# Two attention layers' openings and last slots rearranged: key rows, key tiles, mask branch, score banks, copies

## The chip, the cores and the metric

One core of one Trainium2 chip runs the kernel in one launch. The metric is the device time of an execution in microseconds; lower is better. Within an execution the hardware profiler's trace gives every instruction's start and length.

## The reference

Four residual steps over x of 8 batches x 256 tokens x 128 features, in float32:

```
x = x + attention_0(layernorm(x), ctx, ctx)       # 16 heads of 8 features, with biases, softmax
x = x + experts(layernorm(x))                     # top-1 of 8 experts, 128 -> 512 -> 128, silu, times the gate
x = x + attention_1(layernorm(x), ctx, ctx)       # no biases; scores get -slope[h] * (pos_q - pos_k), and
                                                  # -inf where mask == 0; e = exp(s - max s); e / (1 + sum e)
x = x + spikes(layernorm(x))                      # relu(x Wfc)^2 Wproj, 5 steps of a threshold, counted / 5
```

The mask of the inputs is all ones; the kernel tests it when it runs and has code for both cases.

## The kernel before

Every engine has one instruction stream, written out by hand, and semaphores order them. An attention layer is a loop of slots s = -3 .. 8 (`slots_loop`, L299), one batch of 256 tokens entering per slot and each batch spread over several slots: in slot s batch s+3 is normalized, batch s+2 gets its queries (and, in layer 0, keys), batch s+1 gets the first score pass, batch s the second score pass and its value products, and batch s-1 its division, output product and addition to X. `new`, `nxt`, `cur`, `old` in the code are these. A slot has eight pairs of heads (`pair(i)`, L428).

The first score pass (`p1`, L347) has query rows on partitions; VectorE takes each row's maximum from PSUM (`reduce`, L805, L809, 16 a batch). The negated maxima are split into parts, turned by TensorE (`m_turn`, L408), copied (`m_copy`, L667, to `mT`) and put by a DMA of SP into rows 3, 7, .. of the query tile (`rows_of_maximum`, L1047), so that the second pass (`p2`, L355), with key rows on partitions, yields scores less the maximum. ScalarE takes the exponential from PSUM (L664, 16 a batch), and TensorE multiplies by the values (`pv`, L396, 4 groups of 16 products). Then `o_copy` (L646), transposes to token rows (L454), the division on VectorE (`o_norm`, L822), the transpose of the result (L487), its copy `aT` (L714), the output product (L503) and the addition to X (L913).

Queries and keys are float16 high and low parts: ScalarE writes the full product and the high part, GpSimd or VectorE the low part, and SP's DMAs copy them to rows of `Qt` and `Kt` (three tiles each, `NBUF`). Row block 3 of `Kt` is a constant (clear, then add of a column of `rows`), row block 3 of `Qt` partly too (`q_const`). In layer 0 all this is done in the slots; at the opening the first keys' high part is issued by ScalarE (L643), and `Kt[1]` and `Kt[2]` are cleared and filled by VectorE (L799, L802). SP waits for `inited` (L1057) in slot -1 before it loads the next part of the context and touches those tiles.

PSUM has eight banks: `R` with six, three for the first pass (`row_bank`) and three for the second (`key_bank`), and `M[0]`, `M[1]` for everything else. In the last slot of a layer (s = 7) there is no first pass.

Layer 1's keys and values are computed ahead: for batches 0 to 2 before the experts, for 3 to 6 after them (`ahead_on_tensor`, L556), for 7 in slot -2. The parts go to HBM by SP (L593, L598) and come back as whole key tiles. After the experts TensorE reads a flag that says whether any mask value is zero, and takes one of two branches, each with the whole attention of layer 1 (L1748 to L1754).

`keep_running` (L333) issues 128x512 products that nobody reads; `FILLS` and several places give their number. After attention 1 the last step runs as `ffn` slots s = -3 .. 7: h of batch s+2, transposes of batch s+3, y of batch s+1, spikes of batch s. Slots -3 and -2 stand inside the attention's last slots (`ffn_start`), the rest behind it (`ffn_loop`). Its normalization's statistics come in parts (`FFN_PARTS`).

## Time and profile before

| | |
|---|---|
| three runs, us | 370.54 (median), 370.26, 373.01 |
| the profiled execution's own time, us | 372.42 |
| its span in the trace, us | 370.5 |
| granted TensorE clock, mean over the span | 0.934 |
| busy: TensorE, VectorE, ScalarE, GpSimd | 86%, 75%, 63%, 40% |
| chain that ended last: TensorE, VectorE, issue, ScalarE, DMA | 44%, 22%, 11%, 11%, 8% |
| VectorE's reductions L809 | 256 x 684 ns = 161.7 us of the engine, 16% of the chain |

Shares of busy time are means over stages. By the trace attention 0 lies from 0 to about 131 us, gate and routing to 148, the experts to 202, attention 1 to 337, and the last step's slots from 331 to 370. TensorE's granted clock is 1.00 (2.4 GHz) or 0.50 (1.2 GHz); a mean between them says for what part of a stretch each held. ACTq, SPq and PEq are the engines' queues, in which DMA issues and register loads stand.

### The profile page before, as it was taken

Reading aid. Unit: us, or ns where it says so; the run is one execution under the profiler, and the core shown is the slowest. Engines: PE = TensorE matmul, PEld = TensorE weight load, DVE = VectorE, ACT = ScalarE, POOL = GpSimd, SP = SyncE. Lnnn points to the kernel's source line nnn. Section 1 sums busy time; section 2 is a strip of 40 time slices with the busy share of each in tenths; the row PEclk is TensorE's granted clock in tenths of the full one; section 3 lists DMA queues with packets and bytes.
Section 4 is the critical chain, followed back from the end, with each engine's and each line's share of the span. In section 5 each row is a group of like instructions: output and inputs, shape, how many; then the busy total and the mean of one; then the engine's idle time right before and its main releaser. Section 6 shows DMA issues by size and latency. Waiting matters only on the chain.

```text
span 370.5 us, 9195 instructions
## 1 busy us (share of the span) xinstructions
PE 318.3 (86%) x3235; PEld 188.7 (51%) x3235; DVE 278.8 (75%) x693; ACT 233.3 (63%) x524; POOL 146.4 (40%) x227
## 2 busy tenths in 40 slices
PE   5798889889988866899998597899988998898993
PEld 2333444444443465599898342344444443347993
DVE  5699999999993648455672339999999998604676
ACT  2138988998888424345555211698898986845652
POOL 3244635366300312875420578355434310354500
PEclk9899999999998876899999788999999996879999
DMA  4224343452422053255551332121221120000111
GB/s 170 71 75 115 105 109 104 112 144 54 152 65 60 3 140 97 50 140 152 134 132 39 96 95 63 51 54 31 66 66 54 25 54 7 6 2 1 36 37 42
DMA packets 33118, 27.89 MB, mean 75 GB/s; under 512 B 4544, under 2 KB 27968, under 8 KB 33072
## 3 DMA queue, kind: packets, MB, share of 16 engines
q1 hardware_dynamic: 30960, 24.07, 22.9%
q0 software_dynamic: 1248, 2.56, 3.2%
q10 hardware_dynamic: 864, 0.66, 0.6%
q8 instruction: 28, 0.46, 0.5%
q14 instruction: 18, 0.15, 0.1%
HBM read 14.75 MB, written 5.70 MB: 55 GB/s over the span
## 4 chain that ended last, share of the span: by engine, by line
PE 44%; DVE 22%; issue 11%; ACT 11%; DMA 8%; POOL 2%; ACTq 0%; SPq 0%; DVEq 0%; POOLq 0%
DVE nm L809 16%; PE M L403 13%; ACT Pt L664 7%; PE R L349 6%; PE R L1613 4%; DMA Pt<-in_mask 3%; PE M L1631 3%; PE R L1445 3%; PE R L358 3%; PE R L1428 2%; PE M L336 2%; DMA sorted_y<-ysb 2%; PE M L503 1%; ACT Osb L648 1%; PE R L336 1%
## 5 line engine op out<-in xcount | busy, mean ns | idle before, releaser
L809 DVE TENSOR_REDUCE nm<-R 128x2 f32<-128x512 f32 x256 | 161.7, 684 | 8.6 <-PE R L349 7.3
L664 ACT ACTIVATE Pt<-R 128x512 f32<-128x512 f32 x256 | 140.2, 596 | 32.9 <-PE R L358 31.6
L403 PE MATMUL M<-Pt,Vt 128*32 128x256 f32 x1024 | 73.2, 407 | 0.3 <-ACT Pt L664 0.3
L349 PE MATMUL R<-Kt,Qt 32*128 32x256 f16 x512 | 50.9, 277 | 13.2 <-DVE nm L809 11.7
L358 PE MATMUL R<-Qt,Kt 32*128 32x256 f16 x512 | 52.1, 281 | 2.6 <-ACT Pt L664 2.3
L1473 ACT ACTIVATE hf<-R,small_in 128x128 f32<-128x128 f32 x92 | 26.3, 367 | 27.9 <-PE R L1428 27.8
L349 PEld LDWEIGHTS R<-Kt,Qt 32*128 32x128 f16 x512 | 14.6, 93 | 54.8 <-DVE nm L809 44.0
L403 PEld LDWEIGHTS M<-Pt,Vt 128*32 128x32 f32 x1024 | 27.8, 114 | 26.6 <-ACT Pt L664 9.1
L1333 POOL DMA_INDIRECT xt<-normed_x,source x23 | 22.8, 992 | 17.2 <-PE M L1436 11.5
L1428 PE MATMUL R<-x_t,w_t 128*128 128x128 f32 x184 | 25.6, 282 | 0.6 <-DVE x_t L1496 0.5
L336 PE MATMUL M<-ones 128*128 128x512 f16 x65 | 22.3, 458 | 3.9 <-issue 3.9
L1445 PE MATMUL R<-w_ff,hf 128*128 x184 | 24.4, 277 | 0.9 <-DVE ysb L1502 0.9
L1340 POOL DMA_INDIRECT w_ff<-sorted_y,slot x16 | 15.4, 966 | 21.0 <-DMA sorted_y<-ysb 16.7
L1445 PEld LDWEIGHTS R<-w_ff,hf 128*128 128x128 f32 x184 | 22.4, 192 | 1.3 <-issue 1.2
L1428 PEld LDWEIGHTS R<-x_t,w_t 128*128 128x128 f32 x184 | 22.3, 192 | 1.3 <-issue 1.0
L685 ACT ACTIVATE xnT<-M 128x256 f32<-128x256 f32 x16 | 6.2, 387 | 22.0 <-PE M L467 18.9
L358 PEld LDWEIGHTS R<-Qt,Kt 32*128 32x128 f16 x512 | 15.3, 93 | 8.6 <-ACT Pt L664 5.6
L1502 DVE COPY ysb<-R 128x128 f32<-128x128 f32 x23 | 6.7, 290 | 17.1 <-PE R L1446 11.9
L771 POOL TENSOR_SCALAR xn<-X,mv,rstd 128x128 f32<-128x128 f32 x24 | 19.0, 797 | 1.3
L987 POOL CAST q_hi<-qf 128x256 f16<-128x256 f32 x12 | 4.8, 398 | 36.8 <-ACT qf L699 21.0
L336 PE MATMUL R<-ones 128*128 128x512 f16 x46 | 16.9, 505 | 2.3 <-DVE ones L1720 1.2
L778 POOL TENSOR_SCALAR ve<-mv 128x2 f32<-128x2 f32 x16 | 3.8, 235 | 35.0 <-DVE mv L755 35.0
(191 smaller groups left out, 526.3 us busy)
## 6 DMA issues: line engine op xcount, KB each, us to landing
w_ff<-in_w SPq DMA_DIRECT2D x8, 512.0 KB, 4.0
Pt<-in_mask SPq DMA_DIRECT2D x8, 256.0 KB
Kt<-k_rows SPq DMA_DIRECT2D x8, 256.0 KB, 2.8
Qt<-q_hi SPq DMA_DIRECT2D x30, 64.0 KB, 1.9
k_rows<-Pt SPq DMA_DIRECT2D x24, 64.0 KB
sorted_y<-ysb SPq DMA_DIRECT2D x23, 64.0 KB
Qt<-q_const SPq DMA_DIRECT2D x16, 64.0 KB, 3.5
Qt<-q_lo SPq DMA_DIRECT2D x16, 64.0 KB, 1.9
```

Source lines behind the costliest of these rows:

```text
L336: pe.matmul(bank, ones16[:, :], ones16[:, :].unsqueeze(1).to_broadcast([P, 4, P]), start=True, stop=True)
L349: mm = pe.matmul(row_bank(b, h)[:, q, :], Qt[b % NBUF][rows_of(h), h // HG, q * P:(q + 1) * P], Kt[b % NBUF][rows_of(h), h // HG, :], star ...
L358: mm = pe.matmul(key_bank(b, 2 * pair + hh)[:, k, :], Kt[b % NBUF][rows_of(h), h // HG, k * P:(k + 1) * P], Qt[b % NBUF][rows_of(h), h // ...
L403: mm = pe.matmul(o_bank(b)[KB * i:KB * i + KB, tile * S:(tile + 1) * S], Vflat[par][:, at:at + KB], Pt[g][:, i, k * S:(k + 1) * S], start= ...
L664: act.activation(Pt[i // 2][:, 2 * j + hh, :], key_bank(b, 2 * i + hh).rearrange("p k n -> p (k n)"), ACT.Exp, scale=1.0 / SC).then_inc(ly ...
L771: i = pool.tensor_scalar(xn[par][:, q, :], X[:, b * QT + q, :], mv[:, q, 0:1], rstd[:, q:q + 1], ALU.subtract, ALU.mult)
L809: v.tensor_reduce(nm[par][:, h // 8, :, h % HG, h // HG % 2], row_bank(b, h), AX.X, ALU.max, negate=True)\
L1333: pool.indirect_dma_start(xt[j % XT_BUFS][:, :], None, xn_dram, bass.IndirectOffsetOnAxis(ap=source[:, j:j + 1].bitcast(U32), axis=0)) \
L1340: pool.indirect_dma_start(yg[:, i, :], None, ys_dram, bass.IndirectOffsetOnAxis(ap=slot[:, i:i + 1].bitcast(U32), axis=0)) \
L1428: mm = pe.matmul(S2[j % H_BUFS // 2][:, j % 2, c // 2, (c % 2) * P:(c % 2 + 1) * P], w1_t[j % X_BUFS][:, c, :], x_t[j % X_BUFS][:, :], sta ...
L1445: pe.matmul(o, hf[j % HF_BUFS][:, c * P:(c + 1) * P], second_weights(e, c), start=(c == 0), stop=False)
L1473: i = act.activation(hf[j % HF_BUFS][:, c * P:(c + 1) * P], S2[j % H_BUFS // 2][:, j % 2, c // 2, (c % 2) * P:(c % 2 + 1) * P], ACT.Silu, ...
```

## The change

SP issues all of layer 0's first key rows, after the first key tile is made, and ScalarE issues the first constant query rows instead; the additions that make `q_const` and `vb` change places. GpSimd clears and fills `Kt[1]` and `Kt[2]`, and SP waits for that in slot -1. VectorE computes the first low query part before it normalizes batch 1. Fewer fillers run in slot -2 of both layers. In slot 7 the second pass uses five banks, and pairs 6 and 7 stand before value groups 0 and 1; `o_copy`, the second `m_copy` and the `aT` copy of that slot (in layer 1 those of slot 8 too) are done by VectorE. Layer 1's ahead products of batches 3 to 6 stand inside the branches; SP issues the first constant query rows before the stores of batches 3 and 4, and the stores of 5 and 6 behind the first queries. The bias addition of slots 0 and later stands before the normalization on GpSimd. The last step's statistics come in parts of 2, 4, 1 and 1 batches instead of 6, 1 and 1, and its slot -1 moves into attention slot 8.

```diff
@@ L215
-INIT_KEYS, INIT_TILES, INIT_SECOND, N_INIT = 11, 14, 18, 20
+INIT_KEYS, INIT_KT, INIT_Q, INIT_TILES = 11, 12, 13, 14
@@ L325
+LAST_RING = (4, 5, 3, 1, 2)
-    return R[:, RING + (H * b + n) % RING, :, :]
+    return R[:, LAST_RING[n % len(LAST_RING)] if b == B - 1 else RING + (H * b + n) % RING, :, :]
+def on_vector(ly, b):
+    return b == B - 2 or b == B - 1 and ly["position"]
@@ L388
-            if b > 0 or i >= 1:
+            if b == B - 1:
+                pe.wait_ge(ly["exp_done"], H * b + (2 * i - 3 if i >= 2 else i - 1))
+                if i == 1:
+                    pe.wait_ge(ly["max_done"], H * B)
+            elif b > 0 or i >= 1:
@@ L426
+            pe.wait_ge(inited, INIT_TILES)
@@ L456
+        if ffn and s == B:
+            ffn_start(ffn, -1)
-            keep_running(pe, M[1][:, :], 16)
+            keep_running(pe, M[1][:, :], 10)
@@ L482
-            keep_running(pe, spare, 12)
+            keep_running(pe, spare, 8)
@@ L535
+            if s == B - 1:
+                pair(6)
-        pair(6)
+        if s != B - 1:
+            pair(6)
+        else:
+            pair(7)
-        if ffn and s == B - 1:
+        if s != B - 1:
+            pair(7)
+        elif ffn:
-        pair(7)
@@ L639
-    if b == -2:
-        act.wait_ge(ly["k_hi"], 1)
-        act.wait_ge(inited, INIT_TILES)
-        for block in (0, 2):
-            act.dma_start(Kt[0][block:P:4, :, :], k_hi[:, :]).then_inc(ly["k_rep"], 16)
@@ L674
-        if old:
+        if old and not on_vector(ly, b - 1):
-        if cur:
+            ffn_start(ffn, -1)
+        if cur and s != B - 1:
@@ L686
+        if s == -2 and ly["bias"]:
+            act.wait_ge(inited, INIT_Q)
+            act.dma_start(Qt[0][3:P:4, :, :], q_const[:, :, :]).then_inc(ly["q_tile"], 16)
@@ L710
-        if old:
+        if old and not on_vector(ly, b - 1):
@@ L734
+        exp(7)
-        exp(7)
@@ L791
+    v.tensor_scalar(q_const[:, :, :], q_const[:, :, :], rows[0:KB, 1:2], None, ALU.add).then_inc(inited, 1)
-    v.tensor_scalar(q_const[:, :, :], q_const[:, :, :], rows[0:KB, 1:2], None, ALU.add).then_inc(inited, 1)
-    for i in range(1, NBUF):
-        v.memset(Kt[i][:, :, :], 0.0).then_inc(inited, 1)
-    v.wait_ge(inited, INIT_SECOND)
-    for i in range(1, NBUF):
-        v.tensor_scalar(Kt[i][:, :, :], Kt[i][:, :, :], rows[:, 0:1], None, ALU.add).then_inc(inited, 1)
@@ L834
+    def o_copy(b, par):
+        v.wait_ge(ly["pv_done"], NG * (b + 1))
+        if b >= 2:
+            v.wait_ge(ly["ot_done"], b - 1)
+        v.tensor_scalar(Osb[par][:, :, :].rearrange("p t n -> p (t n)"), o_bank(b)[:, :],
+                        rows[:, 2:3] if ly["position"] else 0.0, None, ALU.add).then_inc(ly["o_copied"], 1)
+    def last_m_copy():
+        v.wait_ge(ly["mT_done"], 2 * B)
+        v.wait_ge(ly["m_rows"], 16 * (2 * B - 2))
+        v.tensor_copy(mT[1][:, :], M16[0][0:2 * KB, 0:S]).then_inc(ly["mT_copied"], 1)
+    def a_copy(b):
+        v.wait_ge(ly["aT_done"], b + 1)
+        v.wait_ge(ly["op_done"], b)
+        v.tensor_copy(aT[:, :], M[1][:, 0:S]).then_inc(ly["aT_copied"], 1)
@@ L852
+        if old and on_vector(ly, b - 1):
+            o_copy(b - 1, 1 - par)
+        if s == B - 1:
+            last_m_copy()
@@ L865
+            if s == -2 and ly["bias"]:
+                v.wait_ge(ly["q_hi"], 1)
+                v.wait_ge(ly["q_copied"], 1)
+                v.tensor_tensor(q_lo[par][:, :], qf[:, :], q_hi[par][:, :], ALU.subtract).then_inc(ly["q_lo"], 1)
@@ L875
-            if s == -2:
+            if s == -2 and ly["position"]:
-                if ly["bias"]:
-                    v.wait_ge(ly["q_copied"], 1)
-                    v.tensor_tensor(q_lo[par][:, :], qf[:, :], q_hi[par][:, :], ALU.subtract).then_inc(ly["q_lo"], 1)
-                else:
-                    v.scalar_tensor_tensor(q_lo[par][:, :], M[0][:, 0:S], QK / float(np.sqrt(DH)), q_hi[par][:, :],
-                                           ALU.mult, ALU.subtract).then_inc(ly["q_lo"], 1)
-                if ly["position"]:
-                    ahead_on_vector(v, KV_LAST, B)
+                v.scalar_tensor_tensor(q_lo[par][:, :], M[0][:, 0:S], QK / float(np.sqrt(DH)), q_hi[par][:, :],
+                                       ALU.mult, ALU.subtract).then_inc(ly["q_lo"], 1)
+                ahead_on_vector(v, KV_LAST, B)
@@ L901
+        if old and on_vector(ly, b - 1):
+            a_copy(b - 1)
+        if ffn and s == B - 1:
+            ffn_stats(v, 1)
@@ L918
-            ffn_stats(v, s - B + 2)
+            ffn_stats(v, s - B + 3)
@@ L935
+def clear_keys(pool):
+    for i in range(1, NBUF):
+        pool.memset(Kt[i][:, :, :], 0.0).then_inc(cleared, 1)
+    pool.wait_ge(loaded, 16 * N_LOADS)
+    pool.wait_ge(cleared, 4 + NBUF - 1)
+    for i in range(1, NBUF):
+        pool.tensor_scalar(Kt[i][:, :, :], Kt[i][:, :, :], rows[:, 0:1], 0.0, ALU.add, ALU.add).then_inc(cleared, 1)
@@ L978
+                clear_keys(pool)
@@ L996
+        if s >= 0 and nxt and ly["bias"]:
+            pool.wait_ge(ly["ob_made"], 1)
+            pool.tensor_tensor(X[:, (b + 1) * QT:(b + 2) * QT, :], X[:, (b + 1) * QT:(b + 2) * QT, :],
+                               ob[:, :].unsqueeze(1).to_broadcast([P, QT, D]), ALU.add).then_inc(ly["x_biased"], 1)
-        if nxt and ly["bias"]:
+        if s < 0 and nxt and ly["bias"]:
@@ L1040
-        if b > -2:
-            sp.dma_start(tile[block:P:4, :, :], k_hi[:, :]).then_inc(ly["k_rep"], 16)
+        sp.dma_start(tile[block:P:4, :, :], k_hi[:, :]).then_inc(ly["k_rep"], 16)
@@ L1057
-            sp.wait_ge(inited, N_INIT)
+            sp.wait_ge(cleared, 4 + 2 * (NBUF - 1))
@@ L1073
-            sp.dma_start(tile[3:P:4, :, :], q_const[:, :, :]).then_inc(ly["q_tile"], 16)
+            if s != -2:
+                sp.dma_start(tile[3:P:4, :, :], q_const[:, :, :]).then_inc(ly["q_tile"], 16)
@@ L1085
+            if s == -2 and ly["position"]:
+                for j in range(KV_EARLY + 2, KV_LAST):
+                    ahead_high_on_sync(sp, j)
+                    ahead_low_on_sync(sp, j)
@@ L1399
-    for j in range(KV_EARLY, KV_LAST):
+    sp.dma_start(Qt[0][3:P:4, :, :], q_const[:, :, :]).then_inc(ly[1]["q_tile"], 16)
+    for j in range(KV_EARLY, KV_EARLY + 2):
@@ L1538
-FFN_PARTS = (0, B - 2, B - 1, B)
+FFN_PARTS = (0, 2, B - 2, B - 1, B)
-    for s in range(-1, B):
+    for s in range(B):
@@ L1594
-        if b in (1, 4):
-            ffn_root(pool, 1 if b == 1 else 2)
+        if b in (2, 3, 5):
+            ffn_root(pool, (2, 3, 5).index(b) + 1)
-        pool.wait_ge(ff["rstd"], 2 if b < FFN_PARTS[1] else 2 * b - 2 * FFN_PARTS[1] + 4)
+        pool.wait_ge(ff["rstd"], 2 * sum(b >= start for start in FFN_PARTS[1:]) + 2)
@@ L1626
+                pe.wait_ge(ly[1]["o_copied"], B)
+            if s == 0:
@@ L1674
-    sp.wait_ge(inited, INIT_TILES)
+    sp.wait_ge(inited, INIT_KT)
@@ L1747
-    ahead_on_tensor(pe, KV_EARLY, KV_LAST)
+        ahead_on_tensor(pe, KV_EARLY, KV_LAST)
+        ahead_on_tensor(pe, KV_EARLY, KV_LAST)
```

## Rows read from the trace of the kernel before

**Rows 1.** Windows, a middle slot: us; busy PE, PEld, DVE, ACT, POOL; clock; DMA.

```profile
51.00:63.00 12.00, 10.88 (x152) 5.29 (x144) 11.76 (x25) 10.83 (x24) 4.87 (x9) 1.00 0.42 124
```

**Rows 2.** Timeline of layer 0's opening: start us, us, engine, line, what, count.

```profile
6.71 0.44 PE L467 MATMUL M<-first_in,xn 128*128 128x128 f32 x2 [0.66 <-DVE xn L761]
...
8.14 1.51 ACTq L643 DMA_DIRECT2D Kt<-k_hi  x2
...
9.70 0.38 ACT L685 ACTIVATE xnT<-M 128x256 f32<-128x256 f32 x1 [3.05 <-issue]
...
10.91 0.18 POOL L934 MEMSET Vt<- 128x32 f32 x1
...
14.53 0.34 SPq L1029 DMA_DIRECT2D ctxT<-in_ctxT  x1
...
15.69 1.29 DVE L809 TENSOR_REDUCE nm<-R 128x2 f32<-128x512 f32 x2 [1.18 <-PE R L349]
...
20.55 0.70 PE L492 MATMUL M<-ctxT,first_in 128*128 128x256 f32 x2 [0.16 <-ACT qf L699]
```

**Rows 3.** DMA issues from 14.5 to 15.5 us, with size and us to landing.

```profile
ctxT<-in_ctxT SPq DMA_DIRECT2D x1, 128.0 KB, 2.4
```

**Rows 4.** Groups of GpSimd by form: count, busy us, mean ns, idle time before.

```profile
L771 POOL TENSOR_SCALAR xn<-X,mv,rstd 128x128 f32<-128x128 f32 x24 | 19.0, 797 | 1.3
...
L1266 POOL MEMSET b2rows<- 128x1024 f16 x1 | 1.0, 951 | 0.0
...
L1281 POOL TENSOR_SCALAR pos_r<-pos_f,small_in 128x256 f32<-128x256 f32 x1 | 0.5, 476 | 0.1
...
L1267 POOL TENSOR_SCALAR brest<-small_in 128x8 f32<-128x8 f32 x1 | 0.2, 202 | 0.1
```

**Rows 5.** Windows in layer 0's last slot, columns as in rows 1.

```profile
112.00:116.00 4.00, 3.00 (x36) 1.33 (x28) 0.78 (x2) 3.94 (x9) 0.00 (x0) 1.00 0.18 24
...
120.00:122.00 2.00, 2.00 (x24) 0.54 (x17) 1.97 (x13) 0.62 (x2) 0.00 (x0) 0.50 0.03 8
```

**Rows 6.** Timeline of layer 0's last two slots.

```profile
110.30 1.07 PE L403 MATMUL M<-Pt,Vt 128*32 128x256 f32 x16
...
118.52 0.42 DVE L913 TENSOR_TENSOR X<-M,X 128x256 f32<-128x256 f32 x1 [3.47 <-PE M L503]
...
118.95 1.94 PE L403 MATMUL M<-Pt,Vt 128*32 128x256 f32 x16
...
123.33 2.62 POOL L1140 TENSOR_TENSOR rstd_all<-ve_all,mhalf 128x14 f32<-128x14 f32 x1
```

**Rows 7.** Instructions on tile mask_any: TensorE's register load, ns and start.

```profile
L1749 PEldq TENSOR_LOAD <-mask_any x1: 413/413/413, 204.8 to 204.8; - x1
```

**Rows 8.** Chain of waits from 195 us on: start us, us, what.

```profile
205.99 3.95 issue
```

**Rows 9.** Timeline of layer 1's opening.

```profile
202.41 0.16 DVE L1321 TENSOR_SCALAR mask_any<-R 128x1 int32<-128x1 f32 x1 [0.47 <-PE R L1326]
...
209.73 0.62 DVE L1515 SCALAR_TENSOR_TENSOR X<-w_ff,gate,X 128x128 f32<-128x128 f32 x2 [4.35 <-DMA w_ff<-sorted_y,slot]
...
216.33 0.38 PE L467 MATMUL M<-first_in,xn 128*128 128x128 f32 x2
...
229.52 0.71 POOL L991 TENSOR_TENSOR q_lo<-qf,q_hi 128x256 f16<-128x256 f32 x1
...
231.38 0.56 SPq L1052 DMA_DIRECT2D Qt<-mT  x1
...
233.64 0.39 PE L349 MATMUL R<-Kt,Qt 32*128 32x256 f16 x4
```

**Rows 10.** Windows in layer 1's last slot, columns as in rows 1.

```profile
320.00:322.00 2.00, 0.85 (x9) 0.35 (x8) 1.06 (x8) 1.94 (x5) 1.44 (x2) 0.93 0.07 16
...
328.00:330.00 2.00, 2.00 (x29) 0.73 (x22) 0.00 (x0) 0.92 (x4) 0.84 (x2) 0.86 0.00 0
```

**Rows 11.** Timeline of the last step's first products.

```profile
331.56 2.00 PE L1613 MATMUL R<-gT,spiking_in 128*128 128x256 f32 x8
```

## The prediction

> **What bounds the kernel now.** I read the page's slices first, then the windows by stage, then the timeline and the chain of waits around the four places that the change touches. In a middle slot of either attention layer VectorE bounds the work: it is busy 11.76 of 12 us, with the clock at full [rows 1]. Nothing of the change shortens its 16 reductions, so the middle stays as it is. What is left are the two openings and the two last slots, which stand in series with the middle; a microsecond there is a microsecond of the total.
>
> Layer 0's opening: ScalarE issues the two high-key transfers at 8.14, and its copy of the transposed tokens, ready since 7.15, starts only at 9.70; VectorE's first reduction starts at 15.69, just behind twelve fillers on TensorE [rows 2]. The last slots: TensorE is busy 3.00 of 4 us from 112 to 116, with the clock at full, and from 120 to 122 it has half [rows 5]; in layer 1 it has half from 321.72 (0.93 on average over two us, of which 0.85 busy) to 328.56 (0.86 over two us) [rows 10]. Sixteen value products take 1.94 us then, against 1.07 [rows 6]. Layer 1's opening: TensorE's branch, 3.95 us without work after 205.99, then sixteen fillers up to the transposes at 216.33 [rows 8, 9].
>
> **The change part by part.**
>
> *Layer 0's opening.* Without the two issues in its queue ScalarE copies at about 7.2 instead of 9.70, issues one constant transfer behind it (0.7 us, beside TensorE's product), and all that follows is 2.5 us earlier. The low query part now stands ahead of the normalization on VectorE; the order costs nothing, since the root that it waits for comes no sooner. SP takes over two issues and drops one; it starts when the key tile is ready, one microsecond earlier, and is done before the query's high part is. With the query there 2.5 us sooner and four fillers fewer, which ended last, the reductions start at 12.3: 3.4 us earlier. Now the other side. Two clears and two additions for key tiles 1 and 2 go to GpSimd, behind its values clear (ends at 11.09), and SP waits for all of them before the second context part, which it issues at 14.53 before the change [rows 2]. A clear of this size is 0.95 us. The addition has no row. Nearest is one with the same operands (one scalar from a tile, one constant) over 256 columns, 476 ns, against 202 ns for 8: 1.1 ns a column, so 1.33 us for 1024 columns. Far bounds: 0.95 us, as the clear; and 5.3 us, at the rate of the normalization, 797 ns for 128 columns with two scalars from tiles [rows 4]. I take 1.33: GpSimd ends at 11.1 + 1.9 + 2.7 + 0.2 for gaps = 15.9. SP issues the context then, and it lands 2.4 us later [rows 3], at 18.3. The key product, at 20.55 before and else at 17.1, waits for it, and the rest of the slot behind it [rows 2]. Gain 20.55 - 18.3 = **2.2 us**. At 0.95 us it is 3.0; at 5.3 us the context lands at 26.3 and the slot loses 5.7. Also queued behind the clears is GpSimd's root for batch 2, which follows them at once and stands in no later chain than the key product.
>
> A rule speaks against this part. The Trainium skill, GPSIMD Engine Reference, section "Performance versus the Vector engine", has 512 elements in 769 ns for a tight loop and keeps elementwise work on VectorE; an estimate by it, 1.54 us an addition, makes this gain 1.8 us instead of 2.2. No row here has this operation at this size.
>
> *The bias add* moves ahead of the root on GpSimd, in time in which it waits for VectorE's moments: nothing. Without that cover it would cost its own 0.7 us a slot, but on GpSimd, which is no bound there: it is busy 4.87 of 12 us [rows 1].
>
> *Layer 0's last slot.* Five score banks instead of three let TensorE run two pairs ahead; three copies leave ScalarE, whose 16 exponentials (9 us) remain. VectorE has no reductions there. Its 128x512 copy has no row; two reductions over the same input take 1.29 us [rows 2], twice the 128x256 addition 0.84 [rows 6]: 0.7, against ScalarE's 0.60, so the rows of the maxima leave 0.25 us later. The order is then: transposes at 113.6, normalization at 114.4, attention transposes at 115.25, copy by 116.2, output product (0.7 us at full clock) by 117.3, addition to X at 117.4 instead of 118.52 [rows 6]. TensorE would end its last value products some 3 us sooner with the clock at full. But behind that stand VectorE's statistics (unchanged) and GpSimd's root, 2.62 us from 123.33 [rows 6], which hold the gate's normalizations and so the last batch. They gain 118.52 - 117.4. I take **1.2 us**; 0 if the clock falls again.
>
> *Layer 1's opening.* The flag is known at 202.57; its load into TensorE's queue stands at 204.8 now, while products run, and ends 4.7 us before the first filler at 209.94 [rows 7 to 9]. The change puts four batches of key products behind the branch. The load then ends at 203.0 and the products start at 203.0 + 4.7 = 207.7, not 202.4. The clock was at half when work came back from the last gap (sixteen fillers took from 209.94 to the transposes at 216.33), so I price them at 1.8 times, as the value products show [rows 6]: four batches took 3.6 us up to 205.99, so two take 3.3 and are done near 211.1 (209.5 at full clock) instead of 204.2. VectorE's low parts of these two stand ahead of its add for batch 0, which goes from 209.73 to 212.5 [rows 9]. Ten fillers instead of sixteen hide what the batches lose: the transposes come near 216, no loss. But GpSimd's root, twelve gathers and its low query part for batch 1 follow that add in order: 229.52 becomes 232.4 [rows 9]. The low part then lands at 235 and the rows of the maxima, issued at 231.38 before, at 236.1, while slot 0's first products stand at 233.64 [rows 9]. Half a microsecond of slack goes first, and VectorE had two reductions left to do; the loss is **1.8 us**. Bounds: none if the key products run at full clock and the code is there sooner (a gain of 0.6 through the transposes), 3 us if all of it stays at half. SP's constant transfer comes earlier; six store issues of 0.6 us move behind the query's low part, where SP waits for the next high part anyway.
>
> *Layer 1's last slot and the tail.* The same five banks and copies. VectorE normalizes statistics of 4 tiles first instead of 12, so they no longer hold its o-normalization. With the clock at full the 6.84 us at half [rows 10] hold 3.8 us of work: 3.0 less, and 0.4 of lulls. Last value products end near 328.2; the first FFN product was at 331.56 [rows 11]. One further FFN slot moves ahead of the attention's last transposes. It fills lulls around these transposes and makes new ones behind ScalarE's relu and VectorE's copy; an estimate is 0.3 us for it, 0 and 1 being its bounds. The tail behind is unchanged. **3.7 us**; 0.4 if the clock falls again.
>
> Sum: -2.2 - 1.2 + 1.8 - 3.7 = -5.3. The profiled execution took 372.42 us around a span of 370.5; it would take 367.1. That is 1.88 above the median of the three runs, 370.54. Against the median: **365.2 us**.
>
> **The rivals.**
>
> *The clock falls again in the last slots.* For it: it fell both times, behind stretches in which TensorE was idle for a quarter (3.00 busy of 4 us) and over half (0.85 of 2) of the time [rows 5, 10], and the new slot still has lulls while VectorE normalizes. Against: by the order above they shrink to about a fifth of the time. Value products and output product at half clock bring the end back to 331.2 and to where it was in layer 0: -2.2 + 1.8 - 0.4 = -0.8, **369.7 us**. If it falls in one layer only, the time is between.
>
> *The branch ahead of the keys costs nothing.* For it: fillers stood between the keys and the transposes, and six of them go. Against: GpSimd's queue does not pass TensorE's fillers. -2.2 - 1.2 - 0.6 - 3.7 = -7.7: **362.8 us**.
>
> *GpSimd's additions run at the normalization's rate.* Place: GpSimd's queue, 13 to 23.7 us, with SP's context issue behind it. For it: a scalar from a tile, as there. Against: the nearer row. +5.7 - 1.2 + 1.8 - 3.7 = +2.6: **373.1 us**. It decides from 4.0 us an addition on, where the context lands 3.1 us later than the product ran and the sum passes zero.
>
> **How the numbers follow.** Forecast 0.43, with a range of its own of 362.9 to 367.3 (from the bounds 3.0 at the opening, 0 to 3 in layer 1). Clock falls again 0.27; free branch 0.14; slow additions 0.08; two of these losses together, or a dearer branch, 0.08. The range 361.8 to 370.8 leaves out the slow additions, the losses together and a little of either edge. Beyond 1% (366.8 and 374.2; about what a measurement of this kernel can tell from no change): faster 0.38 of the forecast, 0.13 of the free branch and 0.02 of the second case (the clock falls in one layer only): 0.53. Within 1%: 0.05 + 0.01 + 0.25 + 0.05 from slow additions + 0.04 = 0.40. Slower: 0.03 of slow additions with a fallen clock and 0.04 of the rest, 0.07.
>
> **What would show it.** Opening: first reduction near 12.3, GpSimd's second addition ending near 15.9, the key product near 18.3 with a wait for the context. Last slots: granted clock 1.00 throughout and, in layer 1, value products ending 3 us sooner from the slot's start. Layer 1's opening: first key product about 5 us after the flag, batch 0's add about 10 us after it instead of 7.2. Wrong would be: an SP release before 14.5, key products right behind the flag, or a half clock in both last slots.

## The result: 1.5% slower, where 1.4% faster was forecast

| | changed | before, same chip | ratio, 95% interval |
|---|---|---|---|
| first measurement, us | 377.94 (376.05 to 380.14, 4 runs) | 371.53 (4 runs) | 1.0153 (1.0103 to 1.0203) |
| repeated beside e9 to e11 (run e12), us | 377.60 (376.40 to 378.23, 4 runs) | 372.42 (21 runs) | 1.0117 (1.0068 to 1.0166) |

The ratios leave out executions that stand apart as slow; of e6's ten they keep three.

The profiled execution took 380.14 us around a span of 378.0 (before: 372.42 and 370.5), and was the slowest of its four. So I laid the same five marks through four traces of the changed program: this one, the repetition, and two runs (e4, e8 below) that only add work behind its end. A stage ends where one of these starts: the transposes to token rows of slot 5, the output product of slot 8, the mask flag, the transposes of layer 1's slot 6, the last batch's last h product (89.6, 130.2, 202.4, 305.2 and 359.1 us before). In us, against the trace of before:

| stage | forecast | the four traces | mean |
|---|---|---|---|
| layer 0's opening, to slot 5 | -2.2 | +5.6, +3.9, +4.4, +6.0 | +5.0 |
| layer 0's slots 5 to 8 | -1.2 | +2.4, +0.7, -1.1, +0.4 | +0.6 |
| gate, routing, experts | 0 | +0.4, -0.3, -0.1, -0.3 | -0.1 |
| layer 1's opening, to slot 6 | +1.8 | +2.3, +2.1, +5.2, +6.1 | +3.9 |
| layer 1's end, last step | -3.7 | -3.0, -1.2, -3.8, -3.8 | -2.9 |
| sum | -5.3 | | +6.5 |

One trace stands for the kernel before. In e5's, whose two openings are those of before, the first stage is 0.6 us longer and the fourth 1.6; in e2's, whose layer 1 is that of before, the fourth is 0.5 shorter. Differences of that size in a single trace show nothing.

### The profile after

The timeline of layer 0's opening (start us, us, engine, line, what), to be laid beside [rows 2]:

```profile
7.26 0.38 ACT L700 ACTIVATE xnT<-M 128x256 f32<-128x256 f32 x1 [0.64 <-PE M L480]
9.98 0.64 SPq L1137 DMA_DIRECT2D Qt<-q_lo  x1
...
11.04 2.01 POOL L978 MEMSET Kt<- 128x1024 f16 x2
12.42 1.29 DVE L822 TENSOR_REDUCE nm<-R 128x2 f32<-128x512 f32 x2 [0.26 <-PE R L355]
13.24 7.40 POOL L982 TENSOR_SCALAR Kt<-Kt,first_in 128x1024 f16<-128x1024 f16 x2 [0.19 <-POOL Kt L978]
...
24.96 1.29 DVE L822 TENSOR_REDUCE nm<-R 128x2 f32<-128x512 f32 x2 [5.67 <-PE R L355]
```

ScalarE's copy comes 2.4 us sooner and the first reduction 3.3 us sooner, as forecast (12.3). But each addition on GpSimd takes 3.70 us, not 1.33, and VectorE, which before ran reductions one behind the other from 17.7 us on, stands idle for 5.67 us. The chain of waits (start us, us, what) names what it waits for:

```profile
13.24 7.41 POOL Kt L982 x2
20.65 0.02 issue
20.67 2.39 DMA ctxT<-in_ctxT
23.06 0.14 issue
23.19 1.19 PE M L505 x2
24.38 0.54 PE R L355 x4
24.92 0.54 PE R L342
25.46 0.85 PE M L527 x4
```

GpSimd ends, SP issues the context, it lands, the key product runs; and behind it the chain stays on TensorE. The windows (us; busy PE, PEld, DVE, ACT, POOL with counts; clock; DMA) show the idle stretch and what follows:

```profile
18.00:22.00 4.00, 0.29 (x1) 0.00 (x0) 1.25 (x3) 0.09 (x1) 3.81 (x4) 0.50 0.06 10
22.00:26.00 4.00, 2.81 (x11) 1.75 (x11) 1.04 (x2) 0.89 (x2) 2.49 (x4) 0.50 0.29 89
26.00:30.00 4.00, 4.00 (x17) 0.87 (x16) 2.79 (x5) 0.76 (x2) 0.84 (x2) 0.50 0.20 56
```

TensorE is idle for 3.7 of 4 us, and its clock is at half from 14.9 to 31.9 us; before it was at half only from 11.1 to 14.5. The fall comes ahead of the long wait, which starts at 18.3 us. At half clock TensorE is full and VectorE, which should bound these slots, has 2.79 of 4 us.

The chain behind the experts, which answers to [rows 8, 9]:

```profile
210.70 0.17 DVE mask_any L1378
210.87 4.54 issue
215.41 1.22 PE R L580 x2
216.63 0.85 PE R L582 x4
217.48 0.85 PE R L580 x2
218.34 0.87 PE R L582 x4
```

The flag, 4.54 us until the branch delivers, and two batches of products at half clock, 3.8 us: all as forecast (4.7 and 3.3). And the ends, first layer 0's slot 7, then layer 1's (timeline):

```profile
120.85 0.69 DVE L852 TENSOR_SCALAR Osb<-M 128x512 f32<-128x512 f32 x1 [0.87 <-PE M L413]
...
121.59 0.66 PE L465 MATMUL M<-first_in,Osb 128*128 128x128 f32 x4 [0.26 <-DVE Osb L852]
...
124.11 1.23 PE L516 MATMUL M<-second_in,aT 128*128 128x128 f32 x4
...
130.19 2.62 POOL L1197 TENSOR_TENSOR rstd_all<-ve_all,mhalf 128x14 f32<-128x14 f32 x1
...
132.91 1.63 DVE L1179 TENSOR_SCALAR Pt<-X,mv_all,rstd_all 128x128 f32<-128x128 f32 x6 [3.20 <-POOL rstd_all L1197]
...
138.19 1.20 PE L516 MATMUL M<-second_in,aT 128*128 128x128 f32 x4
139.18 0.64 PE L1213 MATMUL R<-first_in,Pt 128*128 128x128 f32 x2
139.43 0.42 DVE L953 TENSOR_TENSOR X<-M,X 128x256 f32<-128x256 f32 x1 [2.63 <-PE M L516]
...
339.34 1.99 PE L1671 MATMUL R<-gT,spiking_in 128*128 128x256 f32 x8
```

VectorE's copy costs 0.69 us (forecast 0.7). From slot 7's transposes to its output product it is 2.5 us, before 3.7: the forecast's 1.2. What follows takes it away, see below.

### The profile page after: what moved, and what is told of

The parts are those of the page before. It is cut to its first block, busy times and chain, and to the rows that moved or that the text cites. A ratio compares the mean times of both kernels' runs of the same rounds, so it can differ in the third digit from the quotient of the medians.

```text
span 378.0 us, 9184 instructions
## 1 busy us (share of the span) xinstructions
PE 321.7 (85%) x3225; PEld 194.1 (51%) x3225; DVE 280.3 (74%) x697; ACT 229.7 (61%) x516; POOL 155.4 (41%) x233
## 4 chain that ended last, share of the span: by engine, by line
PE 43%; DVE 18%; ACT 10%; DMA 10%; POOL 8%; issue 7%; SPq 2%; DVEq 0%; POOLq 0%; ACTq 0%
PE M L413 11%; DVE nm L822 8%; ACT Pt L678 7%; PE R L355 5%; DMA Pt<-in_mask 4%; PE R L1671 4%; PE M L1691 3%; POOL w_ff L1397 3%; PE R L1486 3%; PE R L1503 3%; DMA Qt<-mT 2%; PE R L342 2%; POOL Kt L982 2%; PE M L516 2%; PE R L364 2%
## 5 line engine op out<-in xcount | busy, mean ns | idle before, releaser
L413 PE MATMUL M<-Pt,Vt 128*32 128x256 f32 x1024 | 71.8, 402 | 0.0
L355 PE MATMUL R<-Kt,Qt 32*128 32x256 f16 x512 | 53.2, 288 | 13.2 <-DVE nm L822 8.9
L364 PE MATMUL R<-Qt,Kt 32*128 32x256 f16 x512 | 50.6, 282 | 1.1 <-DMA Qt<-mT 1.1
L413 PEld LDWEIGHTS M<-Pt,Vt 128*32 128x32 f32 x1024 | 27.9, 113 | 25.2 <-ACT Pt L678 8.8
L1390 POOL DMA_INDIRECT xt<-normed_x,source x23 | 22.3, 968 | 17.8 <-PE M L1494 12.5
L1397 POOL DMA_INDIRECT w_ff<-sorted_y,slot x16 | 15.5, 967 | 19.8 <-DMA sorted_y<-ysb 15.5
L342 PE MATMUL M<-ones 128*128 128x512 f16 x59 | 18.4, 411 | 0.0
L1701 ACT ACTIVATE Pt<-R 128x1024 f32<-128x1024 f32 x8 | 8.2, 1024 | 14.9 <-PE R L1671 14.9
L1660 POOL TENSOR_SCALAR xn<-X,mv_all,rstd_all 128x128 f32<-128x128 f32 x16 | 12.6, 795 | 8.6 <-PE R L1679 8.4
```

The lines of the kernel that those rows point to most:

```text
L342: pe.matmul(bank, ones16[:, :], ones16[:, :].unsqueeze(1).to_broadcast([P, 4, P]), start=True, stop=True)
L355: mm = pe.matmul(row_bank(b, h)[:, q, :], Qt[b % NBUF][rows_of(h), h // HG, q * P:(q + 1) * P], Kt[b % NBUF][rows_of(h), h // HG, :], star ...
L364: mm = pe.matmul(key_bank(b, 2 * pair + hh)[:, k, :], Kt[b % NBUF][rows_of(h), h // HG, k * P:(k + 1) * P], Qt[b % NBUF][rows_of(h), h // ...
L413: mm = pe.matmul(o_bank(b)[KB * i:KB * i + KB, tile * S:(tile + 1) * S], Vflat[par][:, at:at + KB], Pt[g][:, i, k * S:(k + 1) * S], start= ...
L1390: pool.indirect_dma_start(xt[j % XT_BUFS][:, :], None, xn_dram, bass.IndirectOffsetOnAxis(ap=source[:, j:j + 1].bitcast(U32), axis=0)) \
L1397: pool.indirect_dma_start(yg[:, i, :], None, ys_dram, bass.IndirectOffsetOnAxis(ap=slot[:, i:i + 1].bitcast(U32), axis=0)) \
```

## The experiments

Ratios are to the kernel before, measured beside each: e1 to e4 on one chip, e5 to e8, e9 to e12 and e13 on three others.

### GpSimd's additions: e1, e2, e3, e9

e1 takes them back:

```diff
 def other_tiles_on_vector(v):
...
+    for i in range(1, NBUF):
+        v.memset(Kt[i][:, :, :], 0.0).then_inc(inited, 1)
+    v.wait_ge(inited, INIT_SECOND)
+    for i in range(1, NBUF):
+        v.tensor_scalar(Kt[i][:, :, :], Kt[i][:, :, :], rows[:, 0:1], None, ALU.add).then_inc(inited, 1)
...
-                        clear_keys(pool)
...
-                    sp.wait_ge(cleared, 4 + 2 * (NBUF - 1))
+                    sp.wait_ge(inited, N_INIT)
```

> The changed kernel, with the clears and additions of key tiles 1 and 2 back on VectorE and SP waiting for them there; all else as changed. Theory (GpSimd's two additions, 3.70 us each, hold SP's context issue and GpSimd's own low part, VectorE starves, and TensorE's clock falls behind it): context issue near 12 to 14 us instead of 20.67, first key product near 17 to 18 us instead of 23.19, no half clock in slots -1 and 0, time 377.9 - 8 = about 370 us. Rival 1 (the twelve taken-out fillers and the new order of the opening let the clock fall, whoever clears the tiles): the context comes early, but the clock is still at half from 15 to 32 us, and 374 to 376 us. Rival 2 (the loss is that of the layers' ends, the opening only shifts them): under 1 us less than the changed kernel, 377 us.

e2 makes the opposite edit on the kernel before.

> The kernel before, with only the clears and additions of key tiles 1 and 2 given to GpSimd and SP's wait moved with them. Theory: the additions take 3.70 us each again, SP's context issue moves from 14.53 to about 20.7 us, the key product from 20.55 to 23.2, and with the starved VectorE and the clock at half the whole is 5 to 6 us slower: 376.5 to 377.5 us. Rival 1 (fewer fillers and the new order are needed for the fall): only the 2.6 us by which the key product is late, 374 us. Rival 2 (not the opening): 371.5 us, as before.

e3 exchanges two statements of the changed kernel:

```diff
-                if s == -1 and ly["bias"]:
-                    sp.wait_ge(cleared, 4 + 2 * (NBUF - 1))
                 if s in CTX_SLOTS and ly["bias"]:
                     context_on_sync(sp, CTX_SLOTS.index(s) + 1)
+                if s == -1 and ly["bias"]:
+                    sp.wait_ge(cleared, 4 + 2 * (NBUF - 1))
```

> The changed kernel, with SP issuing the second context part before it waits for GpSimd's key tiles instead of behind that wait. Theory in its narrow form (the late context is the cause): the first key product goes from 23.19 to about 17.5 us and most of the opening's loss is gone, 372 to 373 us. Rival (the additions hold three more things: SP's transfers into key tile 1 and query tile 1, and GpSimd's own root, normalization and low query part, 23.31 us): the key product is early, but slot 0 starts hardly sooner, and the time is 376 to 377 us.

e9 makes the same addition from another operation:

```diff
-                pool.tensor_scalar(Kt[i][:, :, :], Kt[i][:, :, :], rows[:, 0:1], 0.0, ALU.add, ALU.add).then_inc(cleared, 1)
+                pool.tensor_tensor(Kt[i][:, :, :].rearrange("p g n -> p (g n)"), Kt[i][:, :, :].rearrange("p g n -> p (g n)"),
+                                   rows[:, 0:1].to_broadcast([P, NG * S]), ALU.add).then_inc(cleared, 1)
```

> The changed kernel with GpSimd's two additions written as additions of two tiles, the second being the column repeated (1.89 us for 128x1024 f16 behind the kernel's end, against 3.70 us), all else the same. Theory (SP's release follows GpSimd's end one for one, and slot 0 follows SP): additions end at 17.0 instead of 20.6, context issue at 17.1, key product at 19.5 to 20, layer 0's later slots 3.5 to 4 us earlier than in the changed kernel, about 374 us where the changed one is 378 (ratio to before 1.005). Rival (the place on GpSimd is the fault at any price, as its root and low part stand behind): under 2 us gained.

| | key product, us | opening against before, us | ratio, 95% interval |
|---|---|---|---|
| e1, tiles on VectorE | 18.4 | -0.1 | 0.9954 (0.9912 to 0.9996) |
| e2, before with the clear moved | 22.6 | +5.4 | 1.0118 (1.0034 to 1.0202) |
| e3, context ahead of the wait | 18.6 | +0.5 | 1.0082 (1.0027 to 1.0136) |
| e9, 1.87 us an addition | 19.5 | +1.3 | 1.0011 (0.9980 to 1.0042) |

In these traces the moved clear alone makes the whole loss of the opening, on either base. It comes by dose: with additions of 7.4, 3.7 (e9, its timeline next) and 0 us on GpSimd the opening is 5.0 (mean of four traces), 1.3 and -0.1 us longer than before. In the total time e9's 3.7 us less bring 3.9 us by the ratios, 1.0011 against 1.0117, and 4.8 by the medians (372.78 against 377.60). e2's trace is the shortest of its four executions (374.74 us; median 377.42).

```profile
13.17 3.74 POOL L982 TENSOR_TENSOR Kt<-Kt,first_in 128x1024 f16<-128x1024 f16 x2
```

In e3's trace the early context alone brings nearly all of it, though SP's next issues still stand at 20.14. But that is its fastest execution (371.90 us; median 375.01), and its ratio is 1.3 points above e1's, which the 0.5 us in the opening don't explain. What the early context brings in a usual execution is not shown. Against my expectation, e1's opening is no faster than before, though the key product is where I forecast it (18.3). And its clock was at half from 13.2 to 23.5 us. So the clear was not all.

### What an addition costs on GpSimd: e4, e8

> The changed kernel with operations added behind its end, so its total means nothing: on GpSimd, with VectorE idle, the addition of a column to 128x1024 f16, the same over 512 columns, with a constant instead of the column, over 128x1024 f32, and an f32 addition of two tiles; then the 1024-column addition, a clear and another addition while VectorE runs eight 128x1024 f32 copies from SBUF, and two additions while VectorE runs reductions from PSUM. Theory: the addition costs 3.7 us by itself (3.6 ns a column), 1.85 us for 512 columns, and hardly more beside VectorE. Rival 1 (contention: the opening's 3.70 us is a price beside a busy VectorE): 1.3 to 1.9 us alone and 3.7 beside the copies. Rival 2 (the float16 operand is the cost): f32 takes 1.3 to 1.9 us, f16 3.7. Rival 3 (the column operand is): with a constant 1.3 to 1.9 us.

The timeline of GpSimd in e4. The first row is two additions, of 1024 columns (3.72 us) and of 512 (2.00):

```profile
372.91 5.71 POOL L1761 TENSOR_SCALAR Kt<-Kt,first_in 128x1024 f16<-128x1024 f16 x2 [16.58 <-DVE hf L1633]
378.59 3.63 POOL L1761 TENSOR_SCALAR Kt<-Kt 128x1024 f16<-128x1024 f16 x1
382.19 3.71 POOL L1761 TENSOR_SCALAR Pt<-Pt,first_in 128x1024 f32<-128x1024 f32 x1
385.86 1.90 POOL L1766 TENSOR_TENSOR Pt<-Pt 128x1024 f32<-128x1024 f32 x1
387.86 4.50 POOL L1761 TENSOR_SCALAR Kt<-Kt,first_in 128x1024 f16<-128x1024 f16 x1
392.30 1.49 POOL L1769 MEMSET Kt<- 128x1024 f16 x1
393.77 4.13 POOL L1761 TENSOR_SCALAR Kt<-Kt,first_in 128x1024 f16<-128x1024 f16 x1
398.06 7.38 POOL L1761 TENSOR_SCALAR Kt<-Kt,first_in 128x1024 f16<-128x1024 f16 x2 [0.17 <-DVE nm L1821]
```

It is the price of the operation itself: neither float16, nor the column, nor a busy VectorE makes it (beside VectorE's copies it rises to 4.1 and 4.5 us, beside its reductions it stays at 3.69). It left open what sets it apart from the row that I had used.

> The changed kernel with GpSimd operations added behind its end, VectorE idle, so its total means nothing. The row that priced the addition at 1.1 ns a column multiplied twice; the addition added twice and took 3.6 ns a column, in float16 and float32, with a column and with a constant. In order: multiply twice, add twice over 128x1024 f32, to another tile; both over 256 columns; multiply then add over 256; a copy of 128x1024 f16; an f16 addition of two tiles; an f16 addition of a broadcast column as a two-tile operation. Theory (the arithmetic decides): multiply twice 1.2 us, add twice 3.7; over 256 columns 0.48 against 0.93. Rival 1 (reading and writing the same tile is the cost): both 1.2 us here. Rival 2 (the rate is worse with length): 0.48 against 0.48 at 256, 3.7 against 3.7 at 1024. The last form, at the rate of the f32 addition of two tiles (1.90 us), would do the same fill in 1.9 us.

```profile
376.73 1.12 POOL L1772 TENSOR_SCALAR Pt<-Pt,first_in 128x1024 f32<-128x1024 f32 x1 [16.57 <-DVE hf L1633]
377.94 3.74 POOL L1773 TENSOR_SCALAR Pt<-Pt,first_in 128x1024 f32<-128x1024 f32 x1
381.77 0.48 POOL L1774 TENSOR_SCALAR Pt<-Pt,first_in 128x256 f32<-128x256 f32 x1
382.35 1.14 POOL L1775 TENSOR_SCALAR Pt<-Pt,first_in 128x256 f32<-128x256 f32 x1
383.58 0.41 POOL L1776 TENSOR_SCALAR Pt<-Pt 128x256 f32<-128x256 f32 x1
...
387.37 1.89 POOL L1779 TENSOR_TENSOR Kt<-Kt,first_in 128x1024 f16<-128x1024 f16 x1
```

Multiply twice 1.12 us, add twice 3.74, with the same tiles, column and size. The constant differs (2.0 and 0.0), but multiply by 2.0 and add 0.0 over 256 columns takes 0.41, so the addend 0.0 isn't the cost. The arithmetic decides, and the row of [rows 4] at 1.1 ns a column multiplied twice. Neither a single addition nor a multiplication by one that adds the column was run over 1024 columns.

### The clock in the opening: e7, e10

e7 puts back four fillers in slot -2, e10 puts eight more into slot -1 instead (its expectation says seven; 6, 4, 2 for 2, 1, 1 are eight, and its trace has twelve there against e1's four), both on e1:

```diff
 # e7
-                    keep_running(pe, spare, 8)
+                    keep_running(pe, spare, 12)
 # e10
-        FILLS = {(0, -1): (2, 1, 1, 1, 1, 2, 3, 3), ...
+        FILLS = {(0, -1): (6, 4, 2, 1, 1, 2, 3, 3), ...
```

> The changed kernel with key tiles 1 and 2 on VectorE and, beyond that, twelve fillers instead of eight in layer 0's slot -2. With the tiles alone on VectorE TensorE was idle 1.5 us before its first score product at 12.02, its clock was at half from 13.5 to 23.7 us, VectorE waited four times for half-clock products, and slot 0 began at 26.0 as in the kernel before, though the first reduction came 3.0 us sooner. Theory (the four fillers taken out opened that lull, and the clock behind it cost the gain): no half clock after 14 us, slot 0 begins near 24 us, 2 us faster than with eight fillers. Rival (the second context part, which lands for a key product at 18.4 us, holds the slot whatever the clock): slot 0 begins at 25.5 to 26.0, no gain.

> The changed kernel with key tiles 1 and 2 on VectorE and seven more fillers in layer 0's slot -1: 6, 4, 2 instead of 2, 1, 1 behind pairs 0, 1 and 2, where TensorE waited for VectorE. Four fillers more in slot -2 did not stop the clock from falling at 14.4 us. Theory (the lulls of slot -1 between 12.8 and 16 us let the clock fall, and the half clock is what cost the earlier opening its gain): full clock from 14 us on, slot 0's first second-pass product at 24 us instead of 26, 2 us less than with the tiles alone on VectorE (ratio 0.990). Rival 1 (the clock falls whatever TensorE does there): fillers at half clock take 0.4 us each, slot 0 at 27 to 28, ratio 1.000. Rival 2 (VectorE's own work holds the slot): full clock and slot 0 still at 25.5 to 26.

e7 refutes its theory: ratio 1.0008 (0.9974 to 1.0041) where 2 us less than e1's 0.9954 was expected. Its trace, from one of its three longest executions, has half clock from 14.4 to 28.0 us and the second pass from 27.7 on. e10 confirms the next one: 0.9883 (0.9831 to 0.9936; e1's 0.9954 comes from another chip), no half clock until slot 6, second pass from 23.88 us on, 2.25 us sooner than before (26.13), and the first stage 3.1 us shorter. Slots 5 to 8 give 2.7 of that back in this trace, with half clock from 102.5 to 109.3. The windows of e1, then of e13 (below, with e10's fillers):

```profile
12.00:16.00 4.00, 2.98 (x17) 0.92 (x17) 3.96 (x11) 0.38 (x1) 1.03 (x3) 0.66 0.18 51
16.00:20.00 4.00, 4.00 (x16) 1.51 (x14) 2.81 (x6) 1.13 (x3) 2.18 (x3) 0.50 0.07 21
```

```profile
12.00:16.00 4.00, 3.15 (x20) 1.32 (x20) 3.88 (x12) 0.00 (x0) 0.25 (x2) 1.00 0.24 66
16.00:20.00 4.00, 3.46 (x23) 1.36 (x21) 3.84 (x8) 1.75 (x5) 2.94 (x4) 1.00 0.06 18
```

From 16 us on the clock is at full instead of half, and VectorE is busy 3.84 instead of 2.81 of 4 us. Both traces with the eight fillers (e10, e13) keep full clock through the opening; each of the ten others with the changed opening is at half by 16.9 us.

### The branch: e11

```diff
+            ahead_on_tensor(pe, KV_EARLY, KV_LAST)
             pe.wait_ge(mk["any"], 1)
...
             with pe.If(any_masked == 1):
-                ahead_on_tensor(pe, KV_EARLY, KV_LAST)
                 attention_on_tensor(pe, ly[1], True, ffn)
             with pe.Else():
-                ahead_on_tensor(pe, KV_EARLY, KV_LAST)
```

> The changed kernel with layer 1's key products of batches 3 to 6 back ahead of the branch, all else as changed. Theory (the branch cost what was forecast, 1.8 us): key products right behind the flag, add of batch 0 at 7.2 us after it instead of 9.6, low query part of batch 1 at 27.0 instead of 29.4 us after it, 2 us less than the changed kernel. Rival 1 (the fall of the clock behind the gap takes it back, as slots -1 and 0 are bound by it): no difference. Rival 2 (the ten fillers are too few with the keys ahead): the clock stays at half longer, slower than the changed kernel.

Ratio 1.0003 (0.9962 to 1.0044), median 3.9 us below that of the changed kernel beside it; the add of batch 0 is back at 7.1 us after the flag's start. Twice the forecast. Nine traces hold the products behind the branch. Where the first of them starts 4.6 to 5.0 us after the flag, layer 1's opening loses 2.1 to 3.7 us; where it starts 5.8 to 6.6 us after it, 4.7 to 6.1. One of the latter is e8's:

```profile
215.11 1.22 PE L581 MATMUL R<-ctxT,weights_in 128*128 128x256 f32 x2 [6.65 <-issue]
```

### The last slots alone: e5

The kernel before with the parts L325, L388, L535, L674, L710, L734, L834, L852, L901, L918, L1538, L1594, L1626 of the diff, and slot -1 of the last step moved (in L456).

> The kernel before with only the last slots' part of the change: five banks, pairs 6 and 7 ahead of value groups 0 and 1, the copies on VectorE, the last step's statistics in four parts and its slot -1 in attention slot 8; openings as before. Theory from the traces of the changed kernel and of its two variants (layer 0's end gives 0.3 us, since VectorE's statistics and GpSimd's root hold the gate anyway; layer 1's end gives 2 to 3.5): 2.5 to 3.5 us faster than before, ratio 0.990 to 0.993. Rival 1 (the forecast's terms, 1.2 and 3.7): 4.9 us, 0.987. Rival 2 (the clock falls again in both and takes it back): 0.999.

0.9931 (0.9884 to 0.9978): 2.6 us faster. In its trace layer 0's end is 0.7 us longer, layer 1's 5.2 shorter than in that of before; layer 1's opening, which it doesn't change, is 1.6 longer.

### Together: e6, e13

> The changed kernel with three things undone: key tiles 1 and 2 cleared and filled by VectorE, twelve fillers instead of eight in layer 0's slot -2, and layer 1's key products of batches 3 to 6 ahead of the branch. Theory (each of these three parts costs, the rest of the change gains): opening -2, ends -3, layer 1's opening 0 to -0.6: 5 to 6 us faster than before, ratio 0.985. Rival (the variants' gains are not additive, since the clock falls elsewhere when it doesn't fall here): 0.992 to 0.997, as with the key tiles alone undone (0.9954).

0.9862 (0.9800 to 0.9924), but this rests on three executions, and all ten spread from 364.4 to 373.7 us. Its trace has half clock from 14.2 to 27.9, as e7's.

> The changed kernel with key tiles 1 and 2 on VectorE, seven more fillers in layer 0's slot -1 (6, 4, 2 behind pairs 0, 1 and 2), and layer 1's key products ahead of the branch. Theory (the opening's and the branch's costs stand in series and add): ratio of the kernel with tiles and fillers, 0.9883, less the 1.1 points by which the branch's part alone moved the changed kernel (1.0117 to 1.0003): 0.977, about 364 us. Rival (what the earlier keys save is given back by the clock, which falls in another place of layer 1's opening or last slots): 0.985 to 0.988, as without it.

e13 took 367.47 us (366.79 to 369.29) against 373.61: **0.9852 (0.9812 to 0.9892)**, against 1.0153 and 1.0117 for the changed kernel: faster than both. It is less than the sum of the parts (0.977), so the rival stands, by 0.8 points or 3 us. In its trace layer 1's opening is 1.9 us longer than before, where e11's is 0.5 longer; the rest these traces don't settle. The 17.1 us at half around the gate (125.3 to 142.3) stand in e10's and e11's traces too.

### Repeated: e12

> The changed kernel itself, run again beside its variants, since the profiled execution of it (380.14 us) was the slowest of its four. Theory (the opening's loss is in every execution, and of the 7.5 us between the two profiles 2.4 to 3 us, layer 0's slot 6 at half clock, are chance): ratio 1.010 to 1.015, key product at 23 us again, slot 6 at half clock for 3.4 or 6.8 us. Rival (the slot 6 fall belongs to the change): half clock for 6.8 us in slot 6 again, 1.015 to 1.020.

1.0117, key product 23.1, slot 6 at half for 3.4 us (110.2 to 113.6), in the first trace for 6.8 (110.4 to 117.3). In e4 and e8, the same instructions up to there, the clock did not fall in slot 6. So this fall differs between executions of one program, and the 2.4 us by which the first trace's slots 5 to 8 are longer go with it: the other three have +0.7, -1.1 and +0.4.

## Why the prediction was wrong

*GpSimd's addition*, the step that failed first. "Nearest is one with the same operands" took the operands for what sets the price; it is the arithmetic. Measured 3.70 us, within the bounds (0.95 to 5.3) but 2.8 times the value taken. What I worked out from the price held: GpSimd's end by the same sum is 11.1 + 1.9 + 7.4 + 0.2 = 20.6 (measured 20.65), the context 2.4 us behind it. The Trainium skill, GPSIMD Engine Reference, section "Performance versus the Vector engine", was nearer in advice than in number: its 769 ns for 512 elements stand against 2.00 us for this operation over 512 columns and 1.12 us over 1024 for the one that multiplies. Its advice to keep elementwise work on VectorE the traces bear out: VectorE's addition to the same tile takes 0.44 us (two in 0.88, in the trace of before and in e1's).

The price alone doesn't give the result: with 3.70 in place of 1.33 the forecast's own sum is 2.6 - 1.2 + 1.8 - 3.7 = -0.5. From there to the +6.5 of the traces 2.4 us are missing in the opening, 1.8 in layer 0's last slots, 2.1 in layer 1's opening and 0.8 at layer 1's end.

*"Gain 20.55 - 18.3"*, the second step that failed. It took the slot's gain or loss to be that of the key product. At 23.19 that is a loss of 2.6 us; the stage lost 3.9 to 6.0. With the product at 18.4, as forecast, e1 gained nothing; with full clock besides, e10 gained 2.25 us at slot 0. What decides is whether VectorE is fed, and at half clock it isn't. But the length of the half clock doesn't give the loss by itself: e9 had it for 17.1 us, as the changed kernel's first trace, and lost 1.3. The rival on slow additions decided "from 4.0 us an addition on" by the same arithmetic; at 3.7 the change already lost, here and in layer 1's opening. I had put the clock's fall in the last slots alone.

*Bias add*: no cost seen.

*Layer 0's last slot*: 1.2 us forecast. Counted from slot 7's transposes, the addition to X, GpSimd's root and the gate's first normalizations are indeed those 1.2 us sooner (the normalizations 11.3 instead of 12.5 us after them). Slot 8's output product isn't: 16.6 against 16.7 us. TensorE, done sooner with the values, waits longer for the normalizations, and what follows runs at half clock, from 134.3 to 151.4 us, where before it began at 134.0 with most of the gate's products done; the output product takes 1.20 instead of 0.69 us. Over four traces the stage lost 0.6. That the longer wait lengthens the half clock fits all traces with the new last slots (13.7 or 17.1 us in one piece, against 10.2 in the two with the old ones), e5's among them, which changes no opening; no run tried the wait by itself.

*Layer 1's opening*: place, order and first products were right. The size was half of what came: 3.9 over four traces, 3.9 in e11's medians. The step "the products start at 203.0 + 4.7" took one execution's wait as fixed; from the flag's start to the first product it is 4.6 to 6.6 us. What makes the wait longer in one execution than in another is open.

*Layer 1's end*: 3.7 forecast, 2.9 measured. The clock decides. The stage begins in slot 6, where the kernel before has 6.8 us at half (308.1 to 314.9) besides the 6.8 in the last slot. Windows of 14 us from the start of the last slot, in before, e12 and e4:

```profile
319.00:333.00 14.00, 12.52 (x107) 5.79 (x108) 3.19 (x22) 8.90 (x18) 8.26 (x10) 0.76 0.02 4
```

```profile
326.00:340.00 14.00, 12.98 (x114) 6.17 (x112) 5.47 (x26) 7.91 (x17) 8.70 (x12) 0.76 0.02 5
```

```profile
328.00:342.00 14.00, 12.35 (x126) 7.57 (x125) 5.97 (x27) 9.23 (x19) 9.72 (x13) 1.00 0.02 5
```

Over the thirteen traces with the new last slots the gain follows the half clock in slots 6 and 7: 6.8 and 6.8 us as before, gain 1.2 (e12); 6.8 and 3.4, 3.0 to 3.2 (four traces, the first among them); 6.8 and none, 3.8 (e4, e8); 3.4 and none, 5.0 to 5.3 (six). With the clock as the forecast had it, 3.7 was right, and 0.4 for a clock that falls again was low. That the last slot stays at full clock failed in two of the four.

*The rivals*: none had the sum. "Clock falls again" was right in what happens and wrong in where it counts, which is the opening most of all; "slow additions" had the mechanism with a chance of 0.08, its price (5.3 us) from a row that subtracts and multiplies. Additions and branch both came dearer than forecast, the case that had 0.08 as "two of these losses together, or a dearer branch"; the 0.07 for slower was too little for it.

## What to carry to other kernels

Price an operation on an engine from a row with the same arithmetic, not the same operands and shape alone, and where none exists, let the far bound carry chance. Before an early part of a pipeline is made earlier, ask what fills TensorE in the time that opens: the gain here was there only with eight more fillers, whose traces kept full clock. A queue-wide wait in front of a load (SP's, here) makes everything behind it as late as the last thing waited for; the load can stand ahead of it, as in e3, whose time (1.0082) doesn't yet show what that is worth.

## What the runs showed of the hardware

- GpSimd, 128 partitions (e4, e8): multiply twice by scalars 1.12 us for 1024 columns, add twice 3.74, addition of two tiles 1.90 in float32 and 2.12 in float16, of a tile and a repeated column 1.89. Not expected: one fill in two forms differs by a factor of two (7.40 against 3.74 us for two, after and e9).
- Beside VectorE's copies from SBUF GpSimd's addition takes 4.13 to 4.50 us and its clear 1.49 instead of 1.0; beside reductions from PSUM 3.69 (e4). It works the other way too: VectorE's two 128x128 casts take 1.10 and 1.04 us beside GpSimd's clear of the key tiles (after, e9), 0.25 and 0.21 where that clear isn't there (e1, e10).
- The wait behind the branch, from the flag's start to the first product, varies between executions with the same instructions up to there from 4.7 to 6.6 us (after, e12, e4, e8).
- TensorE's clock falls to half in a stretch of one execution and not in that of another, with the same instructions: in layer 0's slot 6 in two of four traces, in layer 1's last slot in two of four.
